# V of eight tiles between their transposes, weights in pieces, softmax sums in four column groups

## The chip, the cores and the metric

One Trainium2 chip; the program runs on all eight NeuronCores, each on its own two sequences, without traffic between them. The metric is the device time of the slowest core in microseconds (us). Engines are named as in the profile: PE (TensorE, its weight loads apart as PEld), DVE (VectorE), ACT (ScalarE), POOL (GpSimd) and SP (SyncE, which here only issues DMAs).

## The reference, cut to what matters

```python
# layer 0
x = x + layernorm(attn0(layernorm(x)))    # one head of 1024; tril, then softmax over all keys
x = x + layernorm(ffn0(layernorm(x)))     # token shift: sigmoid(xr Wr) * (relu(xk Wk)^2 Wv)
# layer 1
x = x + layernorm(attn1(layernorm(x)))    # 16 heads of 64; h + gelu(A) Wpost
x = x + layernorm(ffn1(layernorm(x)))     # (silu(h Wg) * (h Wu)) Wd, hidden 3072, int weights / 127

# attn0: V goes through the einsum 'bqk,bql->bql': it sums A over k alone, and a softmax row sums
# to 1, so a row of its output is its row of V (times that sum)
# attn1: attn = softmax(q . k / 8) over all 2048 keys; A = attn @ V
```

A core has 2 sequences of 2048 tokens and 1024 features: 32 tiles of 128 tokens, or 8 groups of 512.

## The kernel before

Everything is laid down by hand: each engine runs its instructions in the order in which the builder emits them, and waits for semaphores in that order. `B.after(us, fn)` puts a piece of work off until the builder's own clock has moved on by that much, `B.tick(us)` moves it, and `B.until(table, key)` runs what was put off until a token exists. That clock sets an order and no time.

**Phase A1 (layer 0 attention).** POOL issues three weight loads which also cast f32 to bf16: `a_wqT`, `a_wkT`, `a_wv`. `prep(T)` loads tile T into `r_xa`, takes its statistics on DVE (lines 141, 142, 144), the scale on POOL, applies it on ACT (`r_h`), transposes it on PE (line 209, eight products into `p_t`), and copies it out on DVE (line 213, into `a_h0a`). Eight tiles are prepared first; then PE forms M = WqT WkT (line 370, 128 products), some tiny bias products (389, 393), and the first eight `g_chunk` (line 417). Then `tile_step(T)` for 32 tiles: scores (line 474, as wide as the causal part), their row maximum and exponential, two `g_chunk` for the group ahead, V of the tile (line 518, 16 products into `p_v`, bias added on DVE at line 526 into `r_o`), norm, and the sum with x, stored as x1 (`s_x`). After the last tile three loads `b_wv`, `b_wq`, `b_wk` of 2 MB each (as bf16) are issued by POOL.

**Phase A2 (layer 0 FFN, and q, k, v of layer 1).** For each group G of 512 tokens: four `f_tile` (line 717: r from `b_xr` and `b_fr`, then kv from `b_ka` and `b_fv`), the `keys` of group G+1 (line 710, from `b_xk`), four `v_tile` (717), and eight `qk` (710, with the norm products of line 893). `prep1` reads x1 back through `r_xa`, `mix` makes `b_xk` or `b_xr` on DVE (lines 693, 695), `prep2` normalises the new x for layer 1. `f_tile` adds in `r_xt`, a ring of four tiles, each of which is reloaded (`r_xt<-s_x`) once its last content was stored. `weight_casts` are 24 loads on POOL's queue that turn the int weights of the last FFN into bf16.

**Phase B (layer 1).** `att` yields one step at a time. A step takes two blocks of 128 keys, for 512 queries and two heads: four score products (lines 1087 and 1089, 64 rows each), two exponentials on ACT (`c_pt`, 128 x 1024), and for the two blocks of the step before, each in turn, the products with V (line 1106, two of 64 columns into `p_t`) and with ones (line 1109, two of 64 columns into `p_n`, the softmax sums). 64 jobs (`J`) of 8 steps are 512 steps. The first 64 steps run alone; the other 448 stand between the FFN products of earlier groups (lines 1215, 1272, 1284, 1320). `finish` copies sums and products out of PSUM on DVE (1119, 1120), and takes reciprocals in four pieces (line 1125).

## Time and profile before

| | us |
|---|---|
| median of 3 runs | 3402.72 (3401.41 to 3442.32) |
| profiled execution, its own time | 3405.34 |
| its span (core 1, the slowest) | 3404.3 |
| spans of the eight cores | 3375.8 to 3404.3 |
| PE busy, DVE, ACT, POOL | 3124.2, 1495.5, 1855.1, 650.6 |

All times in what follows are those of core 1 in the profiled execution, counted from its first instruction. Phase A1 runs to about 472 us, A2 to about 1300, B to the end. A busy time is the union of an engine's instructions; the length of one product in a row contains its way through the array, so the pace of products is read from one start to the next.

### The profile page before, as it was taken

What the parts mean: (1) busy time and instruction counts of PE and PEld (TensorE: products, weight loads), DVE (VectorE), ACT (ScalarE), POOL (GpSimd) and SP (SyncE); (2) the same over time, 40 slices, a digit from 0 to 9 for tenths busy, and PEclk for the clock granted to TensorE, in tenths of its full rate; (3) what the DMA queues carried; (4) which work ended last, traced back from release to release, by engine and by line L of the source; (5) the groups of instructions that cost most, each with busy time, mean ns of one, the idle gap of its engine ahead of it and who ended that gap; (6) DMA issues with size and microseconds to landing.
All of it is one profiled execution on the core that took longest, in us unless ns stands there. A gap on an engine that the chain in (4) does not pass through costs nothing.

```text
span 3404.3 us, 50121 instructions; the slowest of 8 cores (3375.8 to 3404.3 us)
## 1 busy us (share of the span) xinstructions
PE 3124.2 (92%) x17414; PEld 1266.2 (37%) x17414; DVE 1495.5 (44%) x2420; ACT 1855.1 (54%) x1948; POOL 650.6 (19%) x1136
## 2 busy tenths in 40 slices
PE   4999984999999997769999999999999999999998
PEld 2444432444444432223333333333333333333333
DVE  2556654655665532233443334344334343343432
ACT  1444431333333326876676676676676776676521
POOL 1335442222233220020030030030030030030121
PEclk9999996999999999889999999999999999999999
DMA  7336576443444233733444344344343343353252
GB/s 167 112 130 165 157 127 137 119 115 109 124 133 111 82 101 89 164 90 111 129 127 141 123 121 132 120 121 135 117 133 129 110 146 122 110 153 116 69 153 93
DMA packets 226551, 421.16 MB, mean 124 GB/s; under 512 B 83712, under 2 KB 108288, under 8 KB 225152
## 3 DMA queue, kind: packets, MB, share of 16 engines
q1 hardware_dynamic: 213936, 378.10, 35.1%
q0 software_dynamic: 12368, 39.85, 7.8%
q8 instruction: 145, 2.38, 0.3%
q14 instruction: 102, 0.84, 0.1%
HBM read 357.06 MB, written 104.86 MB: 136 GB/s over the span
## 4 chain that ended last, share of the span: by engine, by line
PE 76%; DVE 7%; ACT 6%; DMA 6%; issue 4%; POOL 1%; DVEq 0%; SPq 0%; ACTq 0%; POOLq 0%
PE ps L1272 10%; PE ps L1284 10%; PE ps L717 9%; PE ps L1320 8%; PE ps L710 7%; PE p_t L1106 6%; PE ps L1087 6%; PE p_n L1109 5%; ACT c_pt L95 5%; PE ps L474 3%; PE ps L518 3%; PE p_n L417 3%; PE ps L1215 2%; DMA a_wkT<-l_wkT 1%; DMA c_v<-s_v 1%
## 5 line engine op out<-in xcount | busy, mean ns | idle before, releaser
L95 ACT ACTIVATE c_pt<-ps,negm 128x1024 bf16<-128x1024 f32 x1024 | 1075.2, 1110 | 228.3 <-PE ps L1089 224.9
L1106 PE MATMUL p_t<-c_pt,c_v 128*64 128x512 bf16 x2048 | 408.0, 395 | 5.4 <-DVE c_pvs L1120 5.0
L1087 PE MATMUL ps<-c_q,c_k 64*128 64x512 bf16 x1024 | 329.6, 385 | 83.2 <-ACT c_pt L95 67.1
L1109 PE MATMUL p_n<-c_pt,ones 128*64 128x512 bf16 x2048 | 396.4, 383 | 0.0
L1272 PE MATMUL ps<-c_h,c_wg 128*128 128x512 bf16 x1536 | 367.5, 382 | 23.7 <-DMA c_h<-c_h 23.7
L1284 PE MATMUL ps<-c_h,c_wu 128*128 128x512 bf16 x1536 | 364.7, 380 | 0.0
L1320 PE MATMUL ps<-c_wd,c_hh 128*128 128x512 bf16 x1536 | 351.8, 382 | 6.1 <-DVE c_o L1221 4.0
L1089 PE MATMUL ps<-c_q,c_k 64*128 64x512 bf16 x1024 | 331.7, 387 | 0.0
L1278 DVE SCALAR_TENSOR_TENSOR c_th<-c_th,ps 128x512 f32<-128x512 f32 x192 | 132.0, 687 | 415.9 <-ACT c_th L95 415.9
L95 ACT ACTIVATE c_th<-ps 128x512 f32<-128x512 f32 x192 | 114.6, 597 | 294.4 <-PE ps L1272 291.6
L151 POOL TENSOR_SCALAR c_pof<-c_pof 128x1 f32<-128x1 f32 x32 | 6.6, 206 | 1398.1 <-DVE c_pof L144 1398.1
L1290 DVE TENSOR_TENSOR c_hh<-c_th,ps 128x512 bf16<-128x512 f32 x192 | 131.0, 683 | 240.4 <-PE ps L1284 240.4
L1125 DVE RECIPROCAL c_sums<-c_sums 128x128 f32<-128x128 f32 x256 | 227.5, 921 | 0.8 <-DVE c_pvs L1120 0.7
L1272 PEld LDWEIGHTS ps<-c_h,c_wg 128*128 128x128 bf16 x1536 | 138.0, 98 | 236.3 <-issue 94.3
L1320 PEld LDWEIGHTS ps<-c_wd,c_hh 128*128 128x128 bf16 x1536 | 142.7, 98 | 207.9 <-issue 52.2
L1284 PEld LDWEIGHTS ps<-c_h,c_wu 128*128 128x128 bf16 x1536 | 138.7, 98 | 206.9 <-issue 59.9
L1106 PEld LDWEIGHTS p_t<-c_pt,c_v 128*64 128x64 bf16 x2048 | 115.3, 109 | 256.5 <-issue 204.9
L1087 PEld LDWEIGHTS ps<-c_q,c_k 64*128 64x128 bf16 x1024 | 65.5, 94 | 332.9 <-issue 332.8
L209 PE MATMUL p_t<-ident,r_h 128*128 128x128 bf16 x768 | 64.9, 233 | 109.5 <-ACT r_h L95 35.5
L1119 DVE COPY c_sums<-p_n 128x512 f32<-128x512 f32 x64 | 44.0, 687 | 226.9 <-PE p_n L1109 211.6
L1109 PEld LDWEIGHTS p_n<-c_pt,ones 128*64 128x64 bf16 x2048 | 116.9, 110 | 53.4 <-issue 2.0
L95 ACT ACTIVATE b_t<-ps 128x1024 bf16<-128x1024 f32 x60 | 61.0, 1019 | 133.7 <-PE ps L710 129.1
(188 smaller groups left out, 4255.2 us busy)
## 6 DMA issues: line engine op xcount, KB each, us to landing
c_wg<-s_wg SPq DMA_DIRECT2D x192, 256.0 KB, 2.8
c_wu<-s_wu SPq DMA_DIRECT2D x192, 256.0 KB, 3.2
s_x<-r_xt SPq DMA_DIRECT2D x64, 512.0 KB, 3.8
c_k<-s_k SPq DMA_DIRECT2D x64, 512.0 KB, 4.3
c_v<-s_v SPq DMA_DIRECT2D x64, 512.0 KB, 5.5
r_xa<-x SPq DMA_DIRECT2D x32, 512.0 KB, 5.4
r_xt<-x SPq DMA_DIRECT2D x32, 512.0 KB, 3.8
r_xa<-s_x SPq DMA_DIRECT2D x32, 512.0 KB, 4.7
```

The source lines that it names most:

```text
L95: return self.ACT.inc(self.nc.scalar.activation(*a, **k))
L710: ins = nc.tensor.matmul(out, w[:, dc * D + oc * 128: dc * D + (oc + 1) * 128], act[:, dc * TG:(dc + 1) * TG], start=(dc == 0), stop=(dc = ...
L717: ins = nc.tensor.matmul(out, act[:, dc * TG + ti * 128: dc * TG + (ti + 1) * 128], w[:, dc * D + half * 512: dc * D + (half + 1) * 512], ...
L1087: nc.tensor.matmul(bank[:, 0:512], k_[0:64, tc * 128:(tc + 1) * 128], q_[0:64, :], start=True, stop=True, tile_position=(0, 0))
L1089: t = PE.inc(nc.tensor.matmul(bank[:, 512:1024], k_[64:128, tc * 128:(tc + 1) * 128], q_[64:128, :], start=True, stop=True, tile_position= ...
L1106: nc.tensor.matmul(p_o[hd * 64:(hd + 1) * 64, :], v_[:, tc * 128 + hd * 64: tc * 128 + (hd + 1) * 64], p[:, hd * 512:(hd + 1) * 512], tile ...
L1109: ins = nc.tensor.matmul(p_l[hd * 64:(hd + 1) * 64, :], B.ones[:, 0:64], p[:, hd * 512:(hd + 1) * 512], tile_position=(0, hd * 64), **fl)
L1125: DVE.inc(v.reciprocal(self.sums[:, q4 * 128:(q4 + 1) * 128], self.sums[:, q4 * 128:(q4 + 1) * 128]))
L1272: ins = nc.tensor.matmul(pA, self.wg[j][:, dc * 128:(dc + 1) * 128], self.h3[:, dc * TG:(dc + 1) * TG], start=(dc == 0), stop=(dc == DC - 1))
L1278: t1 = B.DVE.inc(nc.vector.scalar_tensor_tensor(th[:], th[:], 1.0, pA, op0=ALU.add, op1=ALU.mult))
L1284: ins = nc.tensor.matmul(pB, self.wu[j][:, dc * 128:(dc + 1) * 128], self.h3[:, dc * TG:(dc + 1) * TG], start=(dc == 0), stop=(dc == DC - 1))
L1320: ins = nc.tensor.matmul(bank, self.hh[:, hc * TG + ti * 128: hc * TG + (ti + 1) * 128], wd[:, k * D + half * 512: k * D + (half + 1) * 51 ...
```

## The change

- A1: `a_wv` is loaded first. V of tiles 0 to 7 is computed in the front, each behind the preparation of the next tile, into eight own buffers (`a_vp`) and over three PSUM banks; `tile_step` computes V for T >= 8 only. `g_chunk` goes through three PSUM banks for groups 0 to 2 instead of group 0 alone.
- Turn of A1 to A2: `f0_wrT` is loaded in steps 28 and 29 (four pieces each) instead of 28 to 31; `l1_wv`, `l1_wq`, `l1_wk` are loaded in 24 pieces of 256 KB, put off by 0.5 + 2.6 n us of the builder's clock. The preparation (`prep1`) of group 1 moves from A2's first group to steps 30 and 31 of A1; `mix(1, "k")` is spread over the first group's `f_tile`s instead of standing in one block behind them. The int weight casts move from groups 0 to 5 to groups 1 to 6.
- B: the softmax sums are four products of 32 columns and 256 queries (`add_up`) instead of two of 64 and 512, and a step's products stand as V, V, sums, sums. `finish` takes half as many reciprocals over [128 x 256], and eight copies of 32 x 256 (`place`) lay them out for the multiplication.

```diff
-    for nm, dst in (("l0_wqT", wqT), ("l0_wkT", wkT), ("l0_wv", wv)):
+    for nm, dst in (("l0_wv", wv), ("l0_wqT", wqT), ("l0_wkT", wkT)):
...
+    def values(T, o, t_of, b=2):
...
+        PE.wait(w_tok["l0_wv"], B.until(h_done, T), *v_free[b])
...
+        DVE.wait(t, t_b, t_of)
+        t = DVE.inc(v.tensor_tensor(o[:], bank, bvb[:], op=ALU.add))
+        v_free[b] = [t]
+        return t
...
     for T in range(8):
         prep(T)
-        B.tick(5.0)
+        B.tick(6.5)
+        if T:
+            vp_tok.append(values(T - 1, vp[T - 1], None, (T - 1) % 3))
+    vp_tok.append(values(7, vp[7], None, 7 % 3))
...
-        b = n_gb % 3 if G == 0 else 0
+        b = n_gb % 3 if G <= 2 else 0
...
+        elif T >= 30:
+            A2.prep1(1, 2 * (T - 30))
+            B.after(5.0, lambda: A2.prep1(1, 2 * (T - 30) + 1))
...
-        if T >= 28:
-            for c in range(2):
-                A2.load("f0_wrT", [B.g_done], 2 * (T % 4) + c)
+        if 28 <= T < 30:
+            for c in range(4):
+                A2.load("f0_wrT", [B.g_done], 4 * (T % 2) + c)
...
-    A2.load("l1_wv", [B.v_done])
-    A2.load("l1_wq", [t_sc[31], B.v_done])
-    A2.load("l1_wk", [t_sc[31], B.v_done])
+    for n in range(24):
+        B.after(0.5 + 2.6 * n, lambda n=n: A2.load(("l1_wv", "l1_wq", "l1_wk")[n // 8], [t_sc[31], B.v_done], n % 8))
...
-                if G == 0:
-                    self.prep1(1, ti)
-                if G < 6:
-                    B.weight_casts(4 * G + ti)
+                if G == 0 and ti == 0:
+                    B.after(2.0, lambda: self.mix(1, "k", 2.0))
+                if 1 <= G < 7:
+                    B.weight_casts(4 * G - 4 + ti)
...
-            for hd in range(2):
-                ins = nc.tensor.matmul(p_l[hd * 64:(hd + 1) * 64, :], B.ones[:, 0:64],
-                                       p[:, hd * 512:(hd + 1) * 512], tile_position=(0, hd * 64), **fl)
+        def add_up(J, tc, k, te):
+            fl, p = pt_free[k]
+            for qd in range(4):
+                ins = nc.tensor.matmul(p_l[qd * 32:(qd + 1) * 32, 0:256], B.ones[:, 0:32],
+                                       p[:, qd * 256:(qd + 1) * 256], tile_position=(0, qd * 32), **fl)
...
+            def place(hd):
+
+                DVE.wait(DVE.tok())
+                for half in range(2):
+                    src = self.rows[hd * 64 + half * 32: hd * 64 + half * 32 + 32, :]
+                    for r in range(2):
+                        DVE.inc(v.tensor_copy(self.sums[hd * 64 + r * 32: hd * 64 + r * 32 + 32,
+                                                        half * 256:(half + 1) * 256], src))
...
-                for a in prev:
-                    weigh(*a)
+                for part in (weigh, add_up):
+                    for a in prev:
+                        part(*a)
```

How the instructions stand is shown at three places. First DVE at the start of the program, before: statistics of a tile (`a_pre<-r_xa`) and the copy of a transposed one (`a_h0a<-p_t`).

```order
L141 BN_STATS a_pre<-r_xa_73 128x6
L142 BN_STATS a_pre<-r_xa_73 128x6
L144 BN_AGGR a_pre<-a_pre 128x2
L213 COPY a_h0a<-p_t 128x8x128
L141 BN_STATS a_pre<-r_xa_74 128x6
L142 BN_STATS a_pre<-r_xa_74 128x6
L144 BN_AGGR a_pre<-a_pre 128x2
L213 COPY a_h0a<-p_t 128x8x128
```

The same place on DVE now (L369 is the bias addition of V):

```order
L213 COPY a_h0a<-p_t 128x8x128
L369 TENSOR_TENSOR a_vp_176<-ps,a_bv 128x1024
L141 BN_STATS a_pre<-r_xa_74 128x6
L142 BN_STATS a_pre<-r_xa_74 128x6
L144 BN_AGGR a_pre<-a_pre 128x2
L213 COPY a_h0a<-p_t 128x8x128
L369 TENSOR_TENSOR a_vp_177<-ps,a_bv 128x1024
```

Before each tile's statistics, and before each copy that PE needs for its next V, there stands now the addition that waits for the V before; PE has the eight transposes and the sixteen products of V in turn (lines 209 and 362, eight times each) ahead of the 128 products of M.

Second, PE inside a step of phase B, before (1272, 1284: the FFN's gate and up):

```order
L1089 MATMUL ps<-c_q_114,c_k_121 128x512
L1106 MATMUL p_t<-c_pt_125,c_v_124 64x512 x2
L1109 MATMUL p_n<-c_pt_125,ones 64x512 x2
L1106 MATMUL p_t<-c_pt_126,c_v_124 64x512 x2
L1109 MATMUL p_n<-c_pt_126,ones 64x512 x2
L1272 MATMUL ps<-c_h_131,c_wg_133 128x512 x8
```

And now:

```order
L1110 MATMUL ps<-c_q_114,c_k_122 128x512
L1127 MATMUL p_t<-c_pt_126,c_v_125 64x512 x2
L1127 MATMUL p_t<-c_pt_127,c_v_125 64x512 x2
L1134 MATMUL p_n<-c_pt_126,ones 32x256 x4
L1134 MATMUL p_n<-c_pt_127,ones 32x256 x4
L1310 MATMUL ps<-c_h_132,c_wg_134 128x512 x8
```

The four products of 64 columns alternated between V and sums; now the step has one more change of shape in it, and eight short products at its end.

Third, POOL at the turn to A2, before (L547 adds the last tiles of A1, L807 the first of A2; `s_wg` is an int weight cast):

```order
L645 DMA b_fr<-f_wrT 128x1024 x2
L645 DMA b_wv<-l_wv 128x8x1024
L645 DMA b_wq<-l_wq 128x8x1024
L645 DMA b_wk<-l_wk 128x8x1024
L534 TENSOR_TENSOR a_post<-a_sm 128x1
```

```order
L547 TENSOR_TENSOR r_xt_78<-r_xt_78,r_o_80 128x1024
L151 TENSOR_SCALAR b_pre<-b_pre 128x1
L153 TENSOR_TENSOR b_pre<-b_pre,mhalf 128x1
L160 TENSOR_SCALAR b_pre<-b_pre 128x1
L1445 DMA s_wg<-f_wg 16x16384
L807 TENSOR_TENSOR r_xt_75<-r_xt_75,r_o_81 128x1024
```

And now, from the addition of the last A1 tile on:

```order
L568 TENSOR_TENSOR r_xt_78<-r_xt_78,r_o_81 128x1024
L667 DMA b_wv<-l_wv 128x1024 x2
L829 TENSOR_TENSOR r_xt_75<-r_xt_75,r_o_79 128x1024
L151 TENSOR_SCALAR b_post<-b_post 128x1
L153 TENSOR_TENSOR b_post<-b_post,mhalf 128x1
L160 TENSOR_SCALAR b_post<-b_post 128x1
L667 DMA b_wv<-l_wv 128x1024
```

The three whole loads are gone from one spot; pieces of one or two (three once) stand between POOL's pieces of work for the first group's tiles, and no cast is among them.

## Rows read from the trace of the kernel before

**Rows 1.** The page, part 1: busy time, share of the span, instructions of each engine

```profile
PE 3124.2 (92%) x17414; PEld 1266.2 (37%) x17414; DVE 1495.5 (44%) x2420; ACT 1855.1 (54%) x1948; POOL 650.6 (19%) x1136
```

**Rows 2.** DMA issues: KB each, us from issue to landing

```profile
a_wqT<-l_wqT POOLq DMA_DIRECT2D x1, 2048.0 KB, 26.3
...
a_wv<-l_wv POOLq DMA_DIRECT2D x1, 2048.0 KB, 62.1
```

**Rows 3.** Timeline of PE, 0 to 190 us: start, us, instruction

```profile
50.08 30.55 PE L370 MATMUL ps<-a_wkT,a_wqT 128*128 128x512 bf16 x128 [5.62 <-DMA a_wkT<-l_wkT]
...
104.55 3.62 PE L518 MATMUL ps<-a_wv,a_h0a 128*128 128x512 bf16 x16
```

**Rows 4.** Timeline of DVE, 0 to 50 and 126 to 146 us

```profile
35.34 0.69 DVE L141 BATCH_NORM_STATS2 a_pre<-r_xa 128x6 f32<-128x512 f32 x1 [3.29 <-DMA r_xa<-x]
...
36.85 0.67 DVE L213 COPY a_h0a<-p_t 128x1024 bf16<-128x1024 bf16 x1
...
125.47 1.22 DVE L526 TENSOR_TENSOR r_o<-ps,a_bv 128x1024 f32<-128x1024 f32 x1 [2.79 <-PE ps L518]
```

**Rows 5.** Busy times in stretches: us, busy (instructions) by engine, PE clock, DMA share, GB/s

```profile
102.30:181.80 79.50, 76.79 (x480) 38.61 (x481) 52.63 (x108) 35.96 (x55) 36.27 (x74) 1.00 0.42 140
...
472.00:633.50 161.50, 98.98 (x497) 44.91 (x496) 73.75 (x132) 40.23 (x38) 39.22 (x77) 0.80 0.67 139
633.50:729.80 96.30, 91.99 (x467) 41.70 (x466) 59.30 (x98) 34.92 (x32) 27.73 (x52) 0.98 0.47 121
```

**Rows 6.** Timeline of PE, 440 to 660 us

```profile
470.45 1.89 PE L710 MATMUL p_n<-b_xk,b_fk 128*128 128x512 bf16 x8
483.18 6.57 PE L717 MATMUL ps<-b_fr,b_xr 128*128 128x512 bf16 x16 [10.84 <-DMA b_fr<-f_wrT]
...
521.52 0.61 PE L209 MATMUL p_t<-ident,r_h 128*128 128x128 bf16 x8 [3.38 <-DVE b_h L213]
...
569.39 9.59 PE L710 MATMUL ps<-b_xk,b_fk 128*128 128x512 bf16 x32 [10.71 <-DVE b_xk L695]
...
633.49 3.63 PE L717 MATMUL ps<-b_fr,b_xr 128*128 128x512 bf16 x16
```

**Rows 7.** The chain that ended last, 470 to 580 us

```profile
523.79 28.98 DMA r_xt<-s_x
```

**Rows 8.** DMA, 440 to 620 us: packets, MB, share; an issue; POOL's timeline

```profile
q0 software_dynamic: 4112, 9.96, 40.4%
...
b_wk<-l_wk POOLq DMA_DIRECT2D x1, 2048.0 KB, 59.7
...
474.52 1.18 POOL L645 DMA_DIRECT2D b_fr<-f_wrT  x2
```

**Rows 9.** Timeline of PE, 2060 to 2090 us: one attention step

```profile
2062.18 0.41 PE L1106 MATMUL p_t<-c_pt,c_v 128*64 128x512 bf16 x2
2062.41 0.38 PE L1109 MATMUL p_n<-c_pt,ones 128*64 128x512 bf16 x2
2062.63 0.38 PE L1106 MATMUL p_t<-c_pt,c_v 128*64 128x512 bf16 x2
2062.85 0.38 PE L1109 MATMUL p_n<-c_pt,ones 128*64 128x512 bf16 x2
2063.16 1.90 PE L1284 MATMUL ps<-c_h,c_wu 128*128 128x512 bf16 x8
```

**Rows 10.** Timeline of PE: tiny products at 82 us, products of 32 columns at 607 us

```profile
82.06 1.79 PE L393 MATMUL p_n<-a_bqkb,a_wqT 128*128 128x1 bf16 x64
...
607.70 0.39 PE L893 MATMUL p_n<-b_t,ones 128*32 128x512 bf16 x2
608.02 3.63 PE L710 MATMUL ps<-b_h,b_wq 128*128 128x512 bf16 x16
```

**Rows 11.** PE's waits, 1700 to 3150 us; then busy times in 1440 to 1480

```profile
PE ps L1087 <- ACT c_pt L95: 27.0, 54, 1.2
...
1440.00:1480.00 40.00, 26.30 (x188) 9.17 (x184) 10.55 (x14) 38.85 (x39) 0.00 (x0) 0.95 0.18 60
```

74 lines of the change are left out of this document (43 added, 31 removed).

## The prediction

> **What bounds the kernel now.** The page comes first: PE is busy 92% of the span, no other engine above 54% [rows 1]. So an edit is worth what it takes out of PE's own work, or out of the places where PE stands still. Busy times by stretch show where those are: from 472 to 633.5 us PE works 99 of 161.5 us, at a mean clock of 0.80, while the next group of the same loop takes 96.3 us with 92 busy [rows 5]. The timeline of PE names two more: until 50.08 us it waits for weights [rows 3], and in the first 64 attention steps ACT is the full engine (38.85 of 40 us) and PE is not (26.30) [rows 11]. In the 1450 us of mixed attention and FFN the listed waits of PE are short; the largest, for ACT, is 27.0 us in 54 pieces [rows 11]. There only the number and the pace of products count. I take the change in the three places it touches.
>
> **Part 1, V in the front.** Before, the three weights land one after the other: the first 26.3 us after its issue at 3.3 us, the third 62.1 us after its issue at 5.3 [rows 2]; M starts at 50.08 when the second is there [rows 3]. Now the second and third are the ones that M needs, so M can't start before some 67 us. But eight V come first on PE, and I think that they set its start, through DVE. By the order, DVE has for each tile: the addition for V of tile n, the statistics of tile n+2, the copy of tile n+1; and PE's V of tile n+1 needs that copy. So one turn of the loop is a sum and nothing in it overlaps: addition 1.33 (1.22 [rows 4] and the hand-over), statistics with their aggregate 1.51 (35.34 to 36.85 [rows 4]), copy 0.67 [rows 4], some 0.2 for two semaphores, and V itself, 16 products at the 0.216 us that full 512-column products take (0.22 from one pair to the next [rows 9]) = 3.45. That is 7.15 us a tile. V of tile 0 starts when its weight lands, at about 28.5 (29.6 as before, less one tile load that is now issued later); PE is cold there, as the first M shows (30.55 us where 128 x 0.216 are 27.6 [rows 3]), so it takes 5 us: end at 33.5. Six turns bring V of tile 6 to 76.4. The last turn lacks the statistics: 5.65. V ends and M starts at 82, against 50.08: **32 us later**. M then finds a warm clock and takes 27.6 instead of 30.55: 3 back.
>
> What is taken out later: tile_steps 0 to 7 take 79.5 us, from 102.3 to 181.8, PE busy 76.8 of it [rows 5]. Eight V of 3.45 go: 27.6, which leaves PE 49 us. But the others stay near it: DVE is busy 52.6 less eight additions of 1.22 = 42.8, POOL 36.3 without its gaps [rows 5], and the chain from scores over maximum and exponential to the next scores (PSUM has one score buffer) is covered now by two g_chunks and a transposition, 3.9 us, instead of by 7.4. In the first four steps DVE's 5.35 us a step exceed PE's 4.3 to 5.6. I put one us a step for that: 57 instead of 79.5, **22.5 back**; the third PSUM bank for g_chunk only helps to keep it so. Together the front costs 32 - 3 - 22.5 = **+6.5 us**. Bounds: if DVE and PE hid nothing of the steps, 79.5 - 52 = 27.5 back and an earlier weight, -2; if the steps keep 64 us, +14; and if PE's clock falls in the V loop (a rival below), more.
>
> **Part 2, the turn to A2.** Three things stand in PE's way before: 10.84 us for the last piece of f_wrT, after which the products run at the low clock (6.57 for 16 instead of 3.62); then, from 522 to 569, almost nothing, since a reload of `r_xt` took 28.98 us [rows 6, 7]; and the block of mix behind it (10.71 [rows 6]). The reload was slow because POOL had put 6 MB of weights on the queue at once, the last of which took 59.7 us to land [rows 8], with casts behind them. In the stretch of 180 us the software queue moved 9.96 MB in 40.4% of it, which is 73 us of all 16 engines, 7.3 us a MB [rows 8]; the six MB are 46 us of them whenever they run. Spread over POOL's work of the first group, some 50 us, and with the tile traffic of a normal group beside them (about 0.47 of 96 us [rows 5], half of it in that time), they nearly fill the queues, yet no transfer stands behind more than a piece or two. By need: b_wv when the v_tiles start, 43 us after A2's start, b_wq 57, b_wk 72; POOL passes its pieces at about 17, 42 and 53. That holds, b_wk with the least to spare. f_wrT is now issued one and a half steps earlier, some 25 us ahead of its use. The preparation of group 1 moves into steps 30 and 31: PE 1.8 us more there (four transpositions, 0.61 each with the way through the array [rows 6]), DVE 4 x 2.2 us in a stretch in which it has some 10 of 32 us free, so 2 us more at most. The mix, about 10 us of DVE in the old block, lies between f_tiles in 28 us. And POOL has 24 issues of 0.59 us [rows 8] where three were: 12 us more in the first group. POOL then comes near to 7 us for each f_tile's 7.2, so its chain can make a transposition late by a us or two.
>
> So the first group should take the 96.3 us of its successor [rows 5] and some 8 for the crowd on DVE, POOL and DMA, after 3.8 of extra work ahead of it: 472 + 3.8 + 104 = 580 instead of 633.5: **-53 us**. Bounds: an ideal group, -61; half of the old waiting for the reload back again, -38. The casts that now run in groups 1 to 6 find DMA at a share of 0.47 with casts in it [rows 5]; nothing changes there but the last.
>
> **Part 3, sums in four column groups.** One step in the mixed stretch: V pair at 2062.18, sums 2062.41, V 2062.63, sums 2062.85, FFN 2063.16 [rows 9]. Two products of 64 columns and 512 queries run at the same time: a pair costs 0.22, no more than one would. Where the shape changes (sums to FFN, 0.31), 0.09 to 0.1 is lost; between V and sums, same shape, nothing. Now a sums set is four products of 256. If four overlap as two do, each set is 0.107. Two sets before, 0.43; now 0.215, and one more change of shape, V to sums, 0.095. Gain 0.12 us a step. The issue could limit it: 64 tiny products with their weight loads take 1.79 us [rows 10], under 28 ns each, so four need about 107 ns; that is just the streaming time, and I allow 0.01 a set for friction. Gain **0.1 us a step, 448 steps: -45 us**. The first 64 steps are ACT's [rows 11] and give nothing. On DVE a job loses two reciprocals of 0.92 and half a copy of 0.69, and gets eight copies of 32 x 256. The trace has no such copy; nearest is the 0.69 for 512 columns out of PSUM, so 0.35, and at most 0.69: 2.8 to 5.5 us against 2.2, in a job that has 27 us of PE and more, on an engine with 44% busy [rows 1]. Hidden; the whole trip is needed only a job later. Without that cover it would be 0.6 us a job.
>
> The Trainium skill (TensorEngine Tiling (Array Packing), Key Properties) says that "Changing tiling mode (not just tile) drains the TensorE". The 0.31 against 0.22 [rows 9] agrees. A different page (TensorE: Matmul & The Clock Gate, Part 3) gives 2.38x for three column tiles of 32 and 512 columns; if an efficiency of 0.8 held for the sets here, 0.135 a set, the gain would be 0.065 a step, 29 us instead of 45.
>
> **The sum.** 3405.3 + 6.5 - 53 - 45 = 3314; the median of the runs shown is 2.6 below the profiled execution, so 3311 to 3314: I say **3313**, 2.6% less. The measurement of this kernel can tell about 2% from nothing: 3334.7 is that line, with 22 us to spare.
>
> **Rivals.**
> *Sums gain nothing.* Only two column groups overlap, whatever their width: a set is two pairs of 256, 0.216 as before, and the added change of shape is a pure loss, 448 x 0.095 = +43. 3313 + 45 + 43 = 3401, no change to be seen. For it: the trace only shows two at a time, also with 32 columns (0.32 from the pair at 607.70 to the full product, a change of shape included [rows 10]). Against it: these two differ only in partition group, as the four do, and their 32-column weights overlapped without trouble. Chance 0.17. A half-way result, a set at 0.16, gives 3350: 0.07.
>
> *The V loop runs cold.* PE is idle some 3.1 us in each turn of 7.15. If the clock stays at its low level there, V takes 6.9: seven times 3.45 more, M starts at 106, time 3337. For it: after idle stretches of 10.84 us the clock was low [rows 6]. Against it: after one of 3.38, the eight transpositions at 521.52 took 0.61, not 1.01 [rows 6]. Chance 0.1.
>
> *Slower.* The products of 32 columns don't overlap at all when four groups follow each other, because the weight load of the next has to wait for the product before: a set is 4 x 0.107 = 0.43. A step then costs 0.43 + 0.095 more, 235 us in all: 3313 + 45 + 235 = 3593. It decides from a set of 0.295 on: 0.25 us a step more than before, 113 us, and with parts 1 and 2 the time passes 3471. Against it stand the 32-column pairs of rows 10, which overlap. Chance 0.04.
>
> *The turn gives little.* The pieces come too fast for a DMA that is already near full, a reload waits again: -38 or less instead of -53, 3328 to 3340. Chance 0.1.
>
> **Chances.** Forecast 0.52 (3290 to 3333), turn 0.1, cold 0.1, half-way 0.07, sums nothing 0.17, slower 0.04. The range reaches from 3284 (both bounds of gain in parts 2 and 3) over the cold and the half-way cases to 3375; outside are the useless sums, most of them, and the slow case. Faster by over 2%: the forecast and half of turn and cold, 0.62; within 2%: 0.34; slower 0.04.
>
> **What the new profile would show.** Part 1: M (128 products) starts near 82 us, DVE's additions into `a_vp` 7 us apart; tile_step 8 starts some 6 us later than 181.8. If M starts at 67, DVE is not in lockstep and the front gains 8. Part 2: the first product of the second group's f_tile near 580 + 6 us, no idle of PE over 5 us between, `r_xt` reloads under 10 us. Part 3: the two sums sets of a step 0.11 apart at full clock, the step from its V pair to the FFN product 0.88 us instead of 0.98. What would make me wrong most: the sets at 0.216.

## The result, and the profile after

The changed kernel takes 0.9902 of the time before, 95% interval 0.9882 to 0.9922: some 33 us less, 27 to 40. The forecast was 92 less (3405.3 to 3313). The median of all eight runs of the changed kernel is 3365.56 us. Its profiled execution took 3363.2 us (3405.3 before), and the span of its slowest core, core 4, is 3362.1 (3404.3 before, core 1). In many runs of this program the cores of one die are granted a lower clock; the ratios and the comparisons here leave such runs out.

So that no single core decides, I also read the same five points from PE's timeline on each of the eight cores, and give their mean: start of M, first product of A2, first product of its second group, first attention score, end.

```
us, mean of 8 cores     M      A2     2nd group  attention  end
before                  50.5   481.4  627.2      1287.8     3387.7
after                   96.3   510.0  624.4      1286.2     3352.0
```

The table holds the answer. Of the 36 us by which the mean end is earlier, 34 arise behind the start of attention. Ahead of it, the front's loss and the turn's gain cancel: A2 begins 29 us late, and 39 late if the 10.8 us of waiting at its door before [rows 6] are counted as the turn's.

The page, part 1, of the kernel after (against [rows 1]): PE has 30 us less to do, DVE 67 more, and the bound is still PE.

```profile
PE 3094.2 (92%) x19462; PEld 1214.1 (36%) x19462; DVE 1563.0 (46%) x2804; ACT 1854.1 (55%) x1948; POOL 670.8 (20%) x1157
```

The timeline of PE after, in the front (against [rows 3]; columns start, us, instruction):

```profile
29.05 6.17 PE L362 MATMUL ps<-a_wv,a_h0a 128*128 128x512 bf16 x16 [15.36 <-DMA a_wv<-l_wv]
38.86 6.38 PE L362 MATMUL ps<-a_wv,a_h0a 128*128 128x512 bf16 x16 [3.19 <-DVE a_h0a L213]
...
58.90 4.91 PE L362 MATMUL ps<-a_wv,a_h0a 128*128 128x512 bf16 x16 [3.12 <-DVE a_h0a L213]
...
98.37 27.79 PE L396 MATMUL ps<-a_wkT,a_wqT 128*128 128x512 bf16 x128
...
146.66 0.61 PE L502 MATMUL ps<-a_h0a,a_g 128*128 128x128 bf16 x8 [0.15 <-ACT a_g L95]
...
210.80 4.06 PE L502 MATMUL ps<-a_h0a,a_g 128*128 128x512 bf16 x24 [0.18 <-ACT a_g L95]
```

The idle time in each turn (in brackets) is the forecast one, 3.1 us, and ends with DVE's copy; only ahead of the eighth V it is 1.63. But V itself takes 4.9 to 6.6 us where 3.45 was priced (only the eighth, 3.61 with its way through the array, is at full clock). The turn is 9.4 us on average (29.05 to 94.92 in seven), not 7.15. Steps 0 to 7 take 64.1 us (146.66 to 210.80), not 57. PE's waits there (after the colon: us, times, longest) are for ACT's exponential and normalisation. V no longer stands between the scores; before, the longest wait of these steps was 0.9 us.

```profile
PE ps L502 <- ACT a_e L525: 3.4, 4, 1.3
PE p_t L209 <- ACT r_h L95: 3.4, 1, 3.4
```

Busy times in four stretches (the V loop, steps 0 to 7, A2's first group, its second; against [rows 5]): the granted clock is the third figure from the right. It is 0.76 in the V loop (0.76 to 0.83 on the eight cores). The first group of A2 takes 113.6 us from its first product, where 150.3 were (483.18 to 633.49 [rows 6]; the 161.5 of [rows 5] count the wait ahead of it) and 104 were forecast; its successor takes 96.33, as before.

```profile
28.00:99.00 71.00, 49.53 (x187) 20.18 (x188) 21.44 (x33) 7.45 (x6) 6.02 (x18) 0.76 0.56 124
146.66:210.80 64.14, 53.06 (x352) 27.46 (x353) 44.57 (x99) 33.89 (x55) 33.88 (x72) 0.95 0.48 156
514.57:628.17 113.60, 95.20 (x471) 42.92 (x471) 67.03 (x115) 37.38 (x35) 49.22 (x80) 0.94 0.70 160
628.17:724.50 96.33, 91.76 (x474) 41.96 (x473) 60.73 (x99) 35.17 (x33) 27.80 (x52) 1.00 0.45 121
```

The timeline of PE in A2's first group (against [rows 6]). The three waits of before are gone; what stands in their place is 3.68 for the last of the mix and 9.89 for a normalised tile, each followed by products at the low clock (5.93 for 16 instead of 3.62):

```profile
514.57 1.89 PE L739 MATMUL ps<-b_fr,b_xr 128*128 128x512 bf16 x8 [0.61 <-ACT a_sm L95]
...
549.37 3.31 PE L732 MATMUL ps<-b_xk,b_fk 128*128 128x512 bf16 x8 [3.68 <-DVE b_xk L717]
...
591.98 1.01 PE L209 MATMUL p_t<-ident,r_h 128*128 128x128 bf16 x8 [9.89 <-ACT r_h L95]
592.79 5.93 PE L732 MATMUL ps<-b_h,b_wq 128*128 128x512 bf16 x16
...
628.17 3.63 PE L739 MATMUL ps<-b_fr,b_xr 128*128 128x512 bf16 x16
```

The chain that ended last, 560 to 600 us (against [rows 7]; start, us, what). It is read backwards from the transposition at 591.98. The transposition waited for ACT's normalisation. In ACT's order this stood behind work that needed the buffer of a V tile, and so the store of that tile. That store stood on SP's queue behind a reload, which waited for a store of x, and that again behind another:

```profile
560.89 7.57 DMA s_x<-r_xt
...
568.99 11.73 DMA s_x<-r_xt
...
580.78 0.32 SPq L255
...
581.88 8.63 DMA s_v<-b_vs
...
590.61 1.24 ACT r_h L95
...
591.98 1.01 PE p_t L209 x8
```

One attention step (against [rows 9]). From the V products to the FFN product it is 0.89 us (2063.68 to 2064.57), before 0.98. Two decimals are coarse here: over the 416 steps of each core in which an FFN product follows, the median is 0.888 us in after and 0.987 in before, on the mean of the eight cores, so a step gains 0.099. V and the change to sums take 0.55, the two sets and the change to FFN 0.34. What a set and a change cost apart is read from e7_by_block below: 0.109 and 0.12.

```profile
2063.68 0.62 PE L1127 MATMUL p_t<-c_pt,c_v 128*64 128x512 bf16 x4
2064.23 0.40 PE L1134 MATMUL p_n<-c_pt,ones 128*32 128x256 bf16 x8
2064.57 1.90 PE L1322 MATMUL ps<-c_h,c_wu 128*128 128x512 bf16 x8
```

PE's waits in the mixed stretch, 1700 to 3150 us (against [rows 11]): the wait for ACT's exponential has grown from 27.0 us to 35.0. So 8 us of what the products saved came back as waiting (each on the slowest core of its run).

```profile
PE ps L1108 <- ACT c_pt L95: 35.0, 64, 1.7
```

### The profile page after: what moved, and what is told of

It reads as the page before. It is cut to its first block, busy times and chain, and to the rows that moved or that the text cites. A ratio compares the mean times of both kernels' runs of the same rounds, so it can differ in the third digit from the quotient of the medians.

```text
span 3362.1 us, 54681 instructions; the slowest of 8 cores (3342.5 to 3362.1 us)
## 1 busy us (share of the span) xinstructions
PE 3094.2 (92%) x19462; PEld 1214.1 (36%) x19462; DVE 1563.0 (46%) x2804; ACT 1854.1 (55%) x1948; POOL 670.8 (20%) x1157
## 4 chain that ended last, share of the span: by engine, by line
PE 75%; DVE 8%; ACT 7%; DMA 4%; issue 4%; POOL 1%; DVEq 0%; SPq 0%; ACTq 0%; POOLq 0%
PE ps L1310 10%; PE ps L1322 10%; PE ps L739 9%; PE ps L1358 8%; PE ps L732 7%; PE p_t L1127 7%; PE ps L1108 6%; ACT c_pt L95 4%; PE p_n L1134 4%; PE ps L362 4%; PE ps L502 3%; PE p_n L443 2%; PE ps L1253 2%; DMA c_v<-s_v 1%; PE p_t L209 1%
## 5 line engine op out<-in xcount | busy, mean ns | idle before, releaser
L1127 PE MATMUL p_t<-c_pt,c_v 128*64 128x512 bf16 x2048 | 323.6, 396 | 2.5 <-DVE c_pvs L1145 2.1
L1134 PE MATMUL p_n<-c_pt,ones 128*32 128x256 bf16 x4096 | 208.3, 280 | 0.0
L1159 DVE COPY c_sums<-c_rows 32x256 f32<-32x256 f32 x512 | 179.6, 351 | 25.6 <-DVE c_sums L1159 0.5
L1127 PEld LDWEIGHTS p_t<-c_pt,c_v 128*64 128x64 bf16 x2048 | 72.8, 108 | 198.6 <-issue 198.6
L1134 PEld LDWEIGHTS p_n<-c_pt,ones 128*32 128x32 bf16 x4096 | 62.3, 95 | 215.3 <-issue 215.3
L141 DVE BATCH_NORM_STATS2 c_pof<-c_o 128x6 f32<-128x512 f32 x32 | 22.2, 693 | 233.4 <-ACT c_o L95 233.4
L739 PE MATMUL ps<-b_wv,b_h 128*128 128x512 bf16 x512 | 123.6, 405 | 2.2 <-DVE b_h L213 2.2
L1144 DVE COPY c_rows<-p_n 128x256 f32<-128x256 f32 x64 | 26.9, 420 | 209.8 <-PE p_n L1134 209.7
```

The lines of the kernel that those rows point to most:

```text
L739: ins = nc.tensor.matmul(out, act[:, dc * TG + ti * 128: dc * TG + (ti + 1) * 128], w[:, dc * D + half * 512: dc * D + (half + 1) * 512], ...
L1127: nc.tensor.matmul(p_o[hd * 64:(hd + 1) * 64, :], v_[:, tc * 128 + hd * 64: tc * 128 + (hd + 1) * 64], p[:, hd * 512:(hd + 1) * 512], tile ...
L1134: ins = nc.tensor.matmul(p_l[qd * 32:(qd + 1) * 32, 0:256], B.ones[:, 0:32], p[:, qd * 256:(qd + 1) * 256], tile_position=(0, qd * 32), **fl)
L1159: DVE.inc(v.tensor_copy(self.sums[hd * 64 + r * 32: hd * 64 + r * 32 + 32, half * 256:(half + 1) * 256], src))
```

## The experiments

Each was timed against the kernel before. The means over the cores are read as above; the last column is the ratio.

```
us, mean of 8 cores   M     A2     2nd group  attention  end      ratio
e1_old_front          52.6  476.0  590.8      1254.3     3319.9   0.9776
e2_sums_only          52.5  484.2  631.4      1293.3     3358.6   0.9899
e3_turn_only          52.5  476.4  591.9      1254.9     3357.6   0.9889
e4_front_only         95.5  513.8  656.4      1320.0     3419.3   1.0083
e5_fill               85.8  501.5  616.8      1279.7     3346.8   0.9874
e6_lag4               68.8  484.8  601.0      1262.3     3327.0   0.9798
e7_by_block           94.4  509.2  626.8      1289.8     3446.9   1.0154
e8_late_reload        52.7  476.3  591.1      1269.1     3333.9   0.9820
e9_pieces             52.2  472.9  601.5      1263.3     3366.7   0.9890
e10_casts             52.2  483.4  616.4      1280.9     3387.5   0.9946
e11_wider             52.3  475.3  592.9      1255.6     3320.3   0.9760
e12_vs4               51.6  475.7  590.6      1251.8     3317.9   0.9762
e13_one_weight        50.7  474.1  575.4      1238.1     3302.2   (below)
```

### The three parts alone

**e1_old_front** is the changed kernel with the front of before: weights in the old order, V in the tile steps.

```diff
-    for nm, dst in (("l0_wv", wv), ("l0_wqT", wqT), ("l0_wkT", wkT)):
+    for nm, dst in (("l0_wqT", wqT), ("l0_wkT", wkT), ("l0_wv", wv)):
...
-        if T:
-            vp_tok.append(values(T - 1, vp[T - 1], None, (T - 1) % 3))
-    vp_tok.append(values(7, vp[7], None, 7 % 3))
```

> The changed kernel with the front of before: weights in the old order, V of tiles 0 to 7 back in the steps, g_chunk over three banks for group 0 alone. The turn and the sums stay changed. Theory A (the front cost what the two traces show, M 48 us later, 15 of it back in steps 0 to 7, 6 more lost in steps 8 to 27): the product of A2's first f_tile starts near 478 instead of 514.6, and the time is 3402.7 - 47 - 37 + 4 to 7 = 3325, a ratio to before of 0.977. Rival B (the front is not the loss; the start of A2 is late for another reason, such as the preparation of group 1 in steps 30 and 31 and its load on DVE): A2 still starts after 490 and the time stays above 3340. If the parts don't add up because an earlier A2 meets a fuller DMA, the first group takes more than 120 us.

Measured: 0.9776, interval 0.9759 to 0.9794, median 3328.09 us. The front is the loss, as theory A had it: without it A2 starts at 476.0 and the kernel is 32 us faster in the mean span. The intervals of the two kernels don't touch, and this one is more than 2% faster than the kernel before.

The other three each take one set of hunks of the change alone. **e2_sums_only** is the kernel before with the sums in four column groups and their order:

```diff
+            for qd in range(4):
+                ins = nc.tensor.matmul(p_l[qd * 32:(qd + 1) * 32, 0:256], B.ones[:, 0:32],
+                                       p[:, qd * 256:(qd + 1) * 256], tile_position=(0, qd * 32), **fl)
...
+                for part in (weigh, add_up):
+                    for a in prev:
+                        part(*a)
```

> The kernel before with the last part alone: sums in four column groups, products grouped by shape, the new finish. Theory A: 0.09 us a step over 448 steps, -40 us, less a few for DVE: 3362 to 3366, ratio 0.989. Rival B: the part gives less, since the 37 us by which the rest of the changed kernel is shorter contain other things (a later start of A2, other casts): above 3375, ratio over 0.992.

Measured: 0.9899 (0.9877 to 0.9921). From the first score to the end it is 2065.3 us in the mean, before 2099.9: 35 less, with the same A1 and A2 as before. In the changed kernel it is 34. Theory A.

**e3_turn_only** is before with the pieces, the earlier f_wrT, and the preparation, mix and casts moved:

```diff
+        elif T >= 30:
+            A2.prep1(1, 2 * (T - 30))
+            B.after(5.0, lambda: A2.prep1(1, 2 * (T - 30) + 1))
...
+    for n in range(24):
+        B.after(0.5 + 2.6 * n, lambda n=n: A2.load(("l1_wv", "l1_wq", "l1_wk")[n // 8], [t_sc[31], B.v_done], n % 8))
```

> The kernel before with the turn alone: f_wrT earlier, 24 pieces, the preparation of group 1 in steps 30 and 31, mix between the f_tiles, casts from group 1 on. Theory A: A2 starts at 472 + 5 and its first group takes 114 us as in the changed kernel, so its second starts at 591 instead of 633.5: -42, 3361, ratio 0.9875. Rival B: with V in the steps the queues at the turn are the same, but the DMA is no freer, so the gain is only the reload wait, 25 us: 3378.

Measured: 0.9889 (0.9871 to 0.9908), 3365.28 us. The second group starts 35 us earlier than before, and 33 us are left at the start of attention: theory A's mechanism, with 35 instead of its 42.

**e4_front_only** is before with the new front:

```diff
+    for nm, dst in (("l0_wv", wv), ("l0_wqT", wqT), ("l0_wkT", wkT)):
...
+        if T:
+            vp_tok.append(values(T - 1, vp[T - 1], None, (T - 1) % 3))
+    vp_tok.append(values(7, vp[7], None, 7 % 3))
```

> The kernel before with the front alone: new order of the weights, V of tiles 0 to 7 in the V loop, g_chunk over three banks for groups 0 to 2. Theory A (the front alone costs what undoing it gave back, and half of its loss is the clock): M starts at 96 to 98, A2 at 503 (35 later than 472 less the 7 of the preparation, that stays in A2 here; the wait for f_wrT comes on top), and the time is 32 to 38 us more than before, ratio 1.010. Rival B (the front's loss is partly hidden before the turn: a later A2 finds its queues emptier): less than 20 us more, ratio 1.005.

Measured: 1.0083 (1.0055 to 1.0112), so 28 us more, between the two theories. A2 starts 32 us late, the second group 29. The three parts add up to the whole within some 10 us: 28 - 38 - 34 by the ratios is -44, with the errors of three ratios on it, and the whole is -33; in mean spans they add up to -28 (+31.6, -30.1, -29.1), the whole is -36.

### The front: clock or lockstep

**e5_fill** puts 12 products whose result nobody reads ahead of V of tiles 1 to 7 (2.75 us a turn in the trace, in the gap in which PE waits for DVE). DVE's lockstep stays, only PE's idle time goes.

```diff
+        if 1 <= T < 8:
+            for _ in range(12):
+                nc.tensor.matmul(p_g, B.ident[:], wv[:, 0:512], start=True, stop=True)
```

> The changed kernel with 12 idle products of 512 columns (identity against a part of a_wv, into the bank of p_n, never read) ahead of V of tiles 1 to 7; no result changes. They fill 2.6 of the 3.1 us that PE waits for DVE in each turn of the V loop. Theory A (V is slow there, 4.9 to 6.6 us instead of 3.45, only because the clock falls in the idle stretches): every V takes 3.5, M starts at 82 to 84 instead of 98.4, and the time is 14 to 16 us less, 3350. Rival B (V is slow because DVE, ACT or the DMAs get in its way in memory): V keeps its 6 us, the fillers take twice 2.6 too, and M starts no earlier than 98.

The timeline of PE in this kernel:

```profile
29.55 6.48 PE L365 MATMUL ps<-a_wv,a_h0a 128*128 128x512 bf16 x16 [14.66 <-DMA a_wv<-l_wv]
...
39.67 3.61 PE L365 MATMUL ps<-a_wv,a_h0a 128*128 128x512 bf16 x16 [0.60 <-DVE a_h0a L213]
...
46.85 3.61 PE L365 MATMUL ps<-a_wv,a_h0a 128*128 128x512 bf16 x16 [0.53 <-DVE a_h0a L213]
```

Every V behind the first takes 3.61, and the turns are 7.18 us (39.67 to 46.85): the 7.15 of the forecast. The granted clock is 1.00 from 36 to 85 us. DVE, ACT and the DMAs do the same work there, so rival B falls: the price of the lockstep was right, and the clock was what it left out. M starts 10.5 us earlier, A2 8.5, but the end only 5.2, where theory A said 14 to 16; what takes the rest back behind A2's start was not tried. The ratio is 0.9874 (0.9856 to 0.9891), a little under the 0.9902 of the changed kernel (the intervals overlap), with work added and nothing removed.

**e6_lag4** puts V of a tile behind the preparation of the fourth tile after it, so PE has a stock of tiles and seldom waits for the latest copy.

```diff
-        if T:
-            vp_tok.append(values(T - 1, vp[T - 1], None, (T - 1) % 3))
-    vp_tok.append(values(7, vp[7], None, 7 % 3))
+        if T >= 4:
+            vp_tok.append(values(T - 4, vp[T - 4], None, (T - 4) % 3))
+    for T in range(4, 8):
+        vp_tok.append(values(T, vp[T], None, T % 3))
```

> The changed kernel with V of tile n emitted behind the preparation of tile n+4 instead of n+1, the last four in a row. The additions for V then stand behind the copies that PE needs, so PE and DVE don't take turns. Theory A (lockstep with DVE makes the V loop 7 us a tile and more with the low clock): V starts at 29 and ends near 60, M starts when its weight lands, at 67 to 70 instead of 96, and the time is 25 to 28 us under the changed kernel's, 3335. Rival B (the weights land late because V's tiles load among them, or the steps behind give it back): M at 80 or later, or steps 0 to 7 take more than 64 us; time over 3350.

The timeline of PE:

```profile
39.26 3.62 PE L362 MATMUL ps<-a_wv,a_h0a 128*128 128x512 bf16 x16
45.18 0.61 PE L209 MATMUL p_t<-ident,r_h 128*128 128x128 bf16 x8 [2.31 <-ACT r_h L95]
...
49.52 13.98 PE L362 MATMUL ps<-a_wv,a_h0a 128*128 128x512 bf16 x64
...
65.58 3.61 PE L362 MATMUL ps<-a_wv,a_h0a 128*128 128x512 bf16 x16 [1.63 <-DVE a_h0a L213]
69.03 11.17 PE L397 MATMUL ps<-a_wkT,a_wqT 128*128 128x512 bf16 x51
```

M starts at 68.8 us, 27.5 earlier than in the changed kernel, and the ratio is 0.9798 (0.977 to 0.9826): theory A. From 29 to 69 us the granted clock is 1.00, and PE's waits behind the first V are the 2.31 and 1.63 us shown. The lockstep was avoidable by the order of the calls alone. But it is no better than the old front (0.9776). M is 16 us later than there, and two things hold it at about the same time: the eight V ahead of it, which it follows without a pause on five of the eight cores, and its second weight, for which it waits 1.1 to 4.8 us on the other three. Steps 0 to 7 give back no more than that (64.3 us in the mean, 79.5 with the old front).

### The turn: why 114 us and not 104

The old front is kept in all of these; e8, e11, e12 and e13 are e1_old_front with one edit, e9 and e10 the kernel before with a part of the turn.

**e8_late_reload** defers the reload of x by 14 us, so that SP's queue doesn't stand waiting for the store of the same buffer.

```diff
-            R.load_xt(n + 4)
+            B.after(14.0, lambda: R.load_xt(n + 4))
```

> The changed kernel with the front of before, and the reload of a ring tile (r_xt<-s_x) put off by 14 us of the builder's clock behind the store that it waits for. On SP's queue the store of V no longer stands behind the waits for those stores. Theory A (of the first group's 114 us, some 10 to 12 are SP waiting for x2 stores, then ACT for the V buffer, then PE): the idle of 11.6 us of PE in the first group goes and A2's second group starts 10 us earlier than with the old front (591), time 3318. Rival B (the DMAs are full there, so whatever stands first, the V stores land late): the idle stays within 3 us, 3328.

Measured: 0.982 (0.9789 to 0.9852), beside the 0.9776 of e1_old_front (the intervals overlap by a little; the mean end is 14 us later). The idle time before the transposition is 10.5 us, where it was 11.6, and in 600 to 1340 us PE's waits for the prepared tiles rise from 7.1 to 21.8 us: x comes later in every group. Theory A fell: the reload's place on the queue was not the cause. The row of e1_old_front that this and the next experiments go by:

```profile
PE p_t L209 <- ACT r_h L95: 13.8, 3, 11.6
```

**e9_pieces** is the kernel before with the weights in pieces, the earlier f_wrT and the casts a group later; the preparation and the mix of the second sequence stay in the first group.

```diff
+    for n in range(24):
+        B.after(0.5 + 2.6 * n, lambda n=n: A2.load(("l1_wv", "l1_wq", "l1_wk")[n // 8], [t_sc[31], B.v_done], n % 8))
...
-                if G < 6:
-                    B.weight_casts(4 * G + ti)
+                if 1 <= G < 7:
+                    B.weight_casts(4 * G - 4 + ti)
```

> The kernel before with three things of the turn part alone: the layer 1 weights of phase A2 loaded in 24 pieces over 62 us, the feed-forward f0_wrT pieces issued in tile steps 28 and 29, and the casts of the big weights moved from A2's groups 0 to 5 to its groups 1 to 6. The preparation of the second sequence (prep1(1)) and its mix stay in A2's first group, as before. The turn alone with all its parts gave 0.9889 with the second group at 588 to 595. Theory A: the 48 us of the first group come from the DMA queues (x reloads landing behind 10 MB of software DMAs), so the pieces bring nearly all: A2 starts at 470 to 473 (no extra 7 us in steps 28 to 31), the waits for the x reload are gone, the block of idle time for the mix, 10.7 us, stays, and the second group starts at 590 to 600; 3365 to 3375 us, ratio 0.990. Theory B: the preparation and the mix inside the first group are the larger share; then the second group starts at 610 or later and the ratio is 0.995 or more.

Measured: 0.989 (0.9854 to 0.9926), second group at 601.5: 26 of the 35 us of e3_turn_only. A2 starts at 472.9, 3.5 earlier than with the moved preparation, which is what the latter costs in steps 30 and 31; in the first group it brings 13. PE's waits from 465 to 635 us show the block of mix still there, and a wait for the reload of 10.5 in place of 29:

```profile
PE p_t L209 <- DVE b_h L213: 13.3, 2, 10.5
PE ps L709 <- DVE b_xk L694: 10.7, 1, 10.7
```

**e10_casts** moves the casts alone.

```diff
-                if G < 6:
-                    B.weight_casts(4 * G + ti)
+                if 1 <= G < 7:
+                    B.weight_casts(4 * G - 4 + ti)
```

> The kernel before with one edit: the casts of the big weights go from A2's groups 0 to 5 to its groups 1 to 6. Four casts of 3.8 us of all DMA engines leave the first group. Theory A (the group is bound by DMA traffic that is in front of the x reloads): the layer 1 weights, 10 MB, are still in front, so the gain is at most the 15 us of the casts, and may be nothing, since the casts are issued behind the weights: second group at 620 to 633, 3390 to 3403 us, ratio 0.996 to 1.000. Theory B (the casts are what the first group waits for): second group at 600 or earlier and a ratio of 0.990.

Measured: 0.9946 (0.9922 to 0.9969), 3392.68 us, between the two theories. The second group starts 11 us earlier, 4 of it are lost before attention. The waits of the same stretch, with the 6 MB of weights still in one go: the longest wait is 13.2 us where it was 29.1; the other two are untouched. So four casts of 0.5 MB, a fifth of the 9.96 MB of software traffic there [rows 8], made more than half of it. (The "10 MB" of the expectation is all of that traffic; the layer 1 weights are 6 MB.)

The first row here is before's:

```profile
PE p_t L209 <- DVE b_h L213: 32.5, 2, 29.1
```

and these are e10_casts':

```profile
PE p_t L209 <- DVE b_h L213: 16.1, 2, 13.2
PE ps L717 <- DMA b_fr<-f_wrT: 11.0, 1, 11.0
PE ps L710 <- DVE b_xk L695: 10.7, 1, 10.7
```

The means order the parts of the turn. The first group takes 145.8 us before, 132.9 with the casts moved (e10_casts), 128.6 with pieces and the earlier f_wrT as well (e9_pieces), 115.5 with the preparation and the mix moved too (e3_turn_only). The earlier f_wrT shows ahead of the group: A2 starts 10.5 us earlier in e9_pieces than in e10_casts. So of the 30 us inside the group the casts made 13, the preparation and the mix 13, and the pieces, which the change is named after, some 4, if the parts are taken in this order; another order was not tried.

**e11_wider** spaces the pieces at 3.4 us.

```diff
-        B.after(0.5 + 2.6 * n, lambda n=n: A2.load(("l1_wv", "l1_wq", "l1_wk")[n // 8], [t_sc[31], B.v_done], n % 8))
+        B.after(0.5 + 3.4 * n, lambda n=n: A2.load(("l1_wv", "l1_wq", "l1_wk")[n // 8], [t_sc[31], B.v_done], n % 8))
```

> The old front with the turn and the sums (3328 us measured, 0.9776), and the 24 pieces of the layer 1 weights spaced at 3.4 us instead of 2.6, so that they ask for 82 us instead of 62. In the first group of A2 an idle time of 11.6 us before a mix product stays, because a reload of x lands late while the DMA engines are full. Theory A: less software DMA at a time lets the reload through, the idle time falls to 5 us or less, and the second group starts some 5 us earlier; 3320 to 3325 us, ratio 0.975 to 0.977. Theory B: the last piece of the wk weights lands at about 565 to 575, after the keys' products want it, and the wait is moved there: 3328 us or more.

Measured: 0.976 (0.9713 to 0.9807), not to be told from e1_old_front's. The waits show why: 1.6 us less in the one place, a new one of 3.9 for the weights. Theory B.

```profile
PE p_t L209 <- ACT r_h L95: 12.5, 3, 10.0
PE ps L712 <- DMA b_wk<-l_wk: 3.9, 1, 3.9
```

**e12_vs4** gives the V tiles of A2 four buffers.

```diff
-        self.vs = [B.sb(f"b_vs{i}", D, BF16) for i in range(2)]
+        self.vs = [B.sb(f"b_vs{i}", D, BF16) for i in range(4)]
```

> The old front with the turn and the sums (3328 us measured, 0.9776), and four buffers for the V tiles of phase A2 in place of two. Theory A: the idle time of 11.6 us before a transposition in A2's first group comes over two buffers. SP's queue stands behind three stores of x of about 10 us each (a reload has to wait for the store of its buffer), the V stores are issued behind that, ACT can't write the third V tile before the first is stored, and the normalisation of x that the transposition wants is behind that in ACT's queue. With four buffers ACT never waits for a V store within the group: the idle time falls to 3 us or less, the second group starts at about 581 instead of 591, 3318 us, ratio 0.975. Theory B: the x stores and reloads themselves are what is late (the DMA engines are full), so the wait is moved to the products of the second group or to another transposition: second group at 588 or later, or its f_tiles wait for x; 3325 us or more, ratio 0.977 or more.

Measured: 0.9762 (0.971 to 0.9814), second group at 590.6. ACT's wait of 15.1 us for the store of a V tile is gone, and PE waits as long as before, for a copy of DVE in the preparation of a later tile, whose load of x is behind the same stores on SP's queue. Theory B by the wait and the second group (the ratio is just under its 0.977): a wait was moved, not removed.

```profile
PE p_t L209 <- DVE b_hx L213: 12.1, 1, 12.1
```

The chain that ended last, 470 to 600 us, has the store, SP's queue and the load that this tile needs in a row:

```profile
532.23 10.81 DMA s_x<-r_xt
...
547.46 5.54 SPq L850
553.09 5.25 DMA r_xa<-s_x
```

**e13_one_weight** takes 16 of the 24 pieces away: the products of Q and K in A2 read the V weights, so Q and K have other values in the same work.

```diff
-    for n in range(24):
-        B.after(0.5 + 2.6 * n, lambda n=n: A2.load(("l1_wv", "l1_wq", "l1_wk")[n // 8], [t_sc[31], B.v_done], n % 8))
+    for n in range(8):
+        B.after(0.5 + 2.6 * n, lambda n=n: A2.load("l1_wv", [t_sc[31], B.v_done], n % 8))
...
-        i, bank, t = self.two("l1_wq" if is_q else "l1_wk", self.h2, need, True, p)
+        i, bank, t = self.two("l1_wv", self.h2, need, True, p)
```

> The old front with the turn and the sums (3328 us measured, 0.9776), and only one of the three layer 1 weights of phase A2 loaded: 8 pieces in place of 24. The products of Q and K in A2 use the V weights, so Q and K are computed with other values in the same number and shape of products. Theory A: the 4 MB of software DMA between 545 and 590 us are what the x and V stores wait for. Without them these stores take 4 to 6 us instead of 9 to 11, the idle time of 11.6 us is 3 us or less, the second group starts at 578 to 583 and the time is 3315 to 3320 us, ratio 0.974 to 0.9755. Theory B: the order of the stores and reloads on SP's queue makes the wait whatever else moves: the idle time stays at 8 us or more, the second group at 588 or later, 3325 us or more.

Two of its four runs count, 3308.78 and 3309.82 us, beside 3399.88 for the kernel before, which is 0.973 and has no interval. The second group starts at 575.4: the first group is 101.2 us, and PE's longest wait in it is this:

```profile
PE ps L712 <- DVE b_xk L697: 3.7, 1, 3.7
```

What the DMA view says of the stores, 440 to 640 us, first in e1_old_front (KB, median us to landing):

```profile
s_x<-r_xt SPq DMA_DIRECT2D x12, 512.0 KB, 5.8
...
s_v<-b_vs SPq DMA_DIRECT2D x4, 256.0 KB, 7.3
```

and in e13_one_weight:

```profile
s_x<-r_xt SPq DMA_DIRECT2D x12, 512.0 KB, 4.2
...
s_v<-b_vs SPq DMA_DIRECT2D x8, 256.0 KB, 2.7
```

(The eight stores of V include four of the second group; the four of the first take 2.6 to 2.9.) Theory A, and by more than it said: without 4 MB of software DMA beside the tile traffic the first group is 13.6 us shorter (101.2 for 114.8). The other 1.8 us of the earlier second group are there at A2's start already and are not the edit's. The edit also takes 16 issues of 0.59 us off POOL, which this run can't tell from the traffic; POOL was busy 49 of 100 us there in e1_old_front, and the stores that the chain named land sooner. This also gives the place of what was left of the forecast: with the traffic out of the way the group takes less than the 104 us I had put.

### The sums

**e7_by_block** is the changed kernel with each block's V and sums in turn, so V, sums, V, sums, FFN: two changes of shape more.

```diff
-                for part in (weigh, add_up):
-                    for a in prev:
-                        part(*a)
+                for a in prev:
+                    weigh(*a)
+                    add_up(*a)
```

> The changed kernel with a step's products ungrouped: V, four sums, V, four sums. Two more changes of shape in a step. Theory A (each change of shape empties the array, 0.095 us): a step is 0.19 us longer than the changed kernel's, 448 steps 85 us, of the whole program 3447, so that four column groups without the grouping would be slower than before. Rival B (only the first products of a new shape wait, and the weight loads ahead of them overlap): 0.05 a change, 45 us, 3407.

One step in its timeline:

```profile
2062.77 0.41 PE L1127 MATMUL p_t<-c_pt,c_v 128*64 128x512 bf16 x2
2063.11 0.29 PE L1134 MATMUL p_n<-c_pt,ones 128*32 128x256 bf16 x4
2063.33 0.41 PE L1127 MATMUL p_t<-c_pt,c_v 128*64 128x512 bf16 x2
2063.67 0.29 PE L1134 MATMUL p_n<-c_pt,ones 128*32 128x256 bf16 x4
2063.89 1.90 PE L1322 MATMUL ps<-c_h,c_wu 128*128 128x512 bf16 x8
```

V to sums is 0.34, of which 0.22 is the V pair [rows 9]: 0.12 for the change. One set and the change to FFN take 0.226 us by the median of the steps from 1500 to 3100 us on three cores, two sets and that change 0.335 in after: a set is 0.109, and this change 0.117. So the four groups overlap fully, which the comparison of before and after alone could not show. The whole stretch from the V products to the FFN product is 1.122 us by the median, 0.234 over after's 0.888, which is 0.117 for each of the two added changes, or 105 us in 448 steps. From the first score to the end it takes 2157.1 us, 91 more than with the products grouped (2065.8). The other 14 were hidden: PE's wait for ACT's exponential (1700 to 3150 us) falls from the 35.0 of after to 21.5. The ratio is 1.0154 (1.0125 to 1.0182): theory A. Ungrouped, the four column groups are slower than the kernel before: the grouping is what makes them pay.

## Why the prediction was wrong

Forecast -92 us, measured -33 (27 to 40). 3365 is inside the range given, at its upper part, and outside of the forecast's own 3290 to 3333. Each of the three terms was off to the same side: the front by some 26 us, the turn by 17, the sums by 11.

**The front, +6.5 forecast, +28 alone and +32 in the whole.** This is the step that failed: the turn of the V loop was priced with V at full clock, 3.45 us, and V took 4.9 to 6.6. In the whole, against e1_old_front in the means, A2's start is 34 us later. It is made of: M 43.7 later (32 forecast), M itself 1.9 shorter (3 forecast), steps 0 to 7 shorter by 16.2 (22.5 forecast), and some 9 us in the later steps that I had not seen.
- "V itself ... = 3.45. That is 7.15 us a tile" was right for DVE's part, as e5_fill's 7.18 shows, and wrong for PE's: in a loop in which PE stands still for 3.1 us of each turn the clock fell, and V took up to 6.6. I had this as a rival and put it at 0.1, since one row showed eight transpositions at full clock after one pause of 3.38. One pause between long stretches of work says nothing of a pause in each turn of a loop.
- The first V ends at 35.2, not 33.5, and the turn behind it is longer; with the clock these are the 12 us. e5_fill gives 10.5 of them back.
- Steps 0 to 7 at "57 instead of 79.5": 63.3 in the mean of the cores, and 64.3 in e6_lag4, where no cold V loop comes first. "The others stay near it" was the right worry with too small a price: the chain from scores over maximum and exponential to the next scores is what PE waits for, and I gave it 1 us a step where it is about 1.8. The clock has a part in it, 0.95 there (1.00 before). My bound of 64 held it.
- Of the later steps, steps 16 to 19 became 1.3 or 4 us longer (by the core), where a pause of 1.63 us is followed by products at the low clock (3.57 for 8), and steps 24 to 27 another 1.6. From the first score of step 28 to A2 it is 61.4 us in the mean, 56.6 in e1_old_front. PE's timelines show the clock there too. In after (core 4), pauses of 3.45 and 2.44 us stand ahead of the scores of steps 28 and 31, and the 32 products of these scores take 8.09 and 8.75 us. In e1_old_front (core 2) the pauses are 1.98 and 1.56 us, and the same products take 6.88 and 6.85. What makes the pauses longer with both parts together was not tried.

**The turn, -53 forecast, -36 measured** (means of the second group's start, 627.2 to 590.8 in e1_old_front, 591.9 in e3_turn_only), just short of the bound of 38. A2 starts at 476.0, forecast 475.8. Two errors make up the 17 us. I took 633.5 from the slowest core, and the mean of the eight is 627.2: 6.3 us of that core's luck. The other 10.8 is the first group, 114.8 instead of 104. Here the step that failed is "they nearly fill the queues, yet no transfer stands behind more than a piece or two". With the pieces beside it a store of x took 7.6 and 11.7 us in the chain of after, and such stores stand in a row on SP's queue, as each reload waits for the store of its buffer. e8, e11 and e12 each changed one link of that chain, and 10 to 12 us of waiting stayed there or came back at the next; e13 took the traffic away, and the wait of 11.6 us was gone. The cause of before's long reload was also shared out wrongly: I put it down to the 6 MB issued at once and named the casts only as what stood behind them. With the 6 MB still in one go and only the casts moved (e10_casts) the longest wait fell from 29.1 to 13.2 us. The rival "the turn gives little", 0.1, described this. That POOL would be late by a us or two was not the matter.

**The sums, -45 forecast, -34 measured** (first score to end; -35 alone). The mechanism was right, and so was the price of a step: four groups overlap fully, and the gain is 0.099 us, forecast 0.1. The added change of shape is 0.12 and not 0.095, and the 0.01 a set that I allowed for friction, 0.002 by e7_by_block, made up for it by luck. These are 44 us in 448 steps. Most of what is missing came back as waits for ACT (27.0 to 35.0), on which I had no term, though the rows showed ACT's waits as the largest of that stretch. DVE's eight copies are 0.35 each in the mean, as forecast (0.28 by the median). PE does not wait for them, but ACT does, for 18 us in 19 pieces (12.6 in 7 for the reciprocals before); whether that is part of the 8 us was not tried.

```profile
L1159 DVE COPY c_sums<-c_rows 32x256 f32<-32x256 f32 x512 | 179.6, 351 | 25.6 <-DVE c_sums L1159 0.5
```

The rivals, too, were priced one at a time. The cold loop (+24), the weak turn (+15) and smaller sums came together. I had given no chance to two of them at once, and no single one reaches 3365 by its own cause, so that 3365 lies inside the range is luck.

The version to keep is the turn and the sums with the old front: 3328 us, 0.9776. e11_wider and e12_vs4 can't be told from it.

## What to carry to other kernels

Price a loop of products that waits in each turn at the low clock as well as at the high one, and let the difference be a term of the sum rather than a rival; a stock of inputs a few turns deep (e6_lag4) took away nearly all of the wait, and the clock stayed at 1.00. When a large transfer is cut in pieces and spread, the sum of bytes stays: look for the small stores and reloads that share that time, and at what they stand in line for. When several parts of a change meet in one place, take them out one at a time: here the casts, moved by one group, brought more of the group than the 24 pieces. A gain that is read as the difference of two places of one core carries that core's luck: take it from the mean of the cores.
